# A second copy of K's high rows: by DMA, or by GpSimd from the first

## The reference

```
query = x @ Wq;  keyt = enc @ Wk;  valt = enc @ Wv          # 8 heads of 80
hs    = softmax(query keyt^T / sqrt(80)) valt               # per head, 100 x 718 scores
ca_q1 = (ca^T Wq_ca) at 100 picked rows
ca_hs1 = mha(ca_q1, x, x);  ca_q2 = ca_hs1 @ Wq
ca_hs2 = mha(ca_q2, ca @ Wk_ca, ca @ Wv_ca)                 # only 4 keys
out   = (hs + ca_hs2) @ Wout + b_out + x
```

## Time and profile before

| | |
|---|---|
| median of 3 runs | 1101.1 us (1098.77 to 1110.14) |
| span of the profiled execution, first to last instruction | 1101.6 us |
| time of the profiled execution as the profile has it | 1101.6 us (one core) |
| TensorE busy | 1036.2 us, 94% |
| VectorE, ScalarE busy | 668.4 us (61%), 490.6 us (45%) |
| GpSimd busy | 280.9 us (26%), 208 instructions |
| DMA by SyncE's queue | 181.63 MB, 72.3% of 16 engines' span |
| mean granted TensorE clock | 0.963 of full |

### The profile page before, as it was taken

How to read it: one execution, slowest core, us unless ns; L and a number is a source line. 1 busy time by engine, 2 the same in 40 slices (tenths; PEclk the granted TensorE clock), 3 DMA queues, 4 the chain that set the end, 5 groups by cost and what they waited for, 6 DMA issues and landing times.

```text
span 1101.6 us, 21261 instructions
## 1 busy us (share of the span) xinstructions
PE 1036.2 (94%) x7192; PEld 1011.9 (92%) x7192; DVE 668.4 (61%) x1138; ACT 490.6 (45%) x889; POOL 280.9 (26%) x208
## 2 busy tenths in 40 slices
PE   6998759999989899999999998999999999998998
PEld 5997749999989899999999998999999999898997
DVE  4444356676756656576656674667675676666344
ACT  4443243635454535354545453455544454445110
POOL 0000132323231322323233323142433151415000
PEclk9899779999999999899999998999998999999999
DMA  8676786767887969596969694869695969697255
GB/s 303 219 204 154 166 173 153 182 163 187 170 171 148 196 133 202 119 211 139 193 142 212 138 196 112 207 148 208 145 198 112 206 152 195 142 200 184 66 172 160
DMA packets 155050, 189.51 MB, mean 172 GB/s; under 512 B 78416, under 2 KB 108112, under 8 KB 155024
## 3 DMA queue, kind: packets, MB, share of 16 engines
q1 hardware_dynamic: 151696, 181.63, 72.3%
q10 hardware_dynamic: 3328, 7.54, 2.1%
HBM read 81.15 MB, written 19.74 MB: 92 GB/s over the span
## 4 chain that ended last, share of the span: by engine, by line
PE 70%; DMA 11%; SPq 4%; DVE 2%; ACT 1%; issue 1%; POOL 0%; DVEq 0%; ACTq 0%; POOLq 0%
PE psB L918 23%; PE psS L887 20%; DMA kstack<-kT_l 10%; PE psS L864 6%; PE psT L901 5%; PE psS L1022 4%; PE psT L941 4%; PE psT L947 2%; SPq L677 2%; PE psB L984 2%; SPq L674 1%; PE psB L1002 1%; DVE kT_l L1346 1%; PE psB L996 1%; PE psT L948 1%
## 5 line engine op out<-in xcount | busy, mean ns | idle before, releaser
L887 PE MATMUL psS<-encT_keep,Wk_keep 128*128 128x360 f32 x1440 | 264.1, 338 | 5.9 <-PEq L173 5.3
L887 PEld LDWEIGHTS psS<-encT_keep,Wk_keep 128*128 128x128 f32 x1440 | 247.4, 196 | 6.7 <-issue 5.3
L918 PE MATMUL psB<-PT_h,encN_h 120*128 120x400 f32 x576 | 203.7, 354 | 0.2 <-POOL encN_l L812 0.2
L918 PE MATMUL psB<-PT_l,encN_h 120*128 120x400 f32 x576 | 199.4, 346 | 0.0
L918 PE MATMUL psB<-PT_h,encN_l 120*128 120x400 f32 x576 | 198.5, 345 | 0.0
L1114 ACT ACTIVATE probs<-psS,negmax 100x718 f32<-100x718 f32 x128 | 110.4, 863 | 169.9 <-DVE negmax L1322 146.6
L1346 DVE TENSOR_TENSOR kT_l<-psS,kT_h 128x718 fp32r<-128x718 f32 x80 | 72.4, 905 | 112.0 <-ACT kT_h L1131 111.9
L1131 ACT ACTIVATE kT_h<-psS 128x718 fp32r<-128x718 f32 x80 | 61.7, 771 | 146.9 <-PE psS L887 137.0
L804 POOL TENSOR_TENSOR encT_keep<-encT_raw,encT_keep 128x718 fp32r<-128x718 f32 x45 | 79.4, 1763 | 181.5 <-ACT encT_keep L1137 179.1
L864 PE MATMUL psS<-kstack,qstack_h 120*100 120x360 f32 x256 | 90.7, 354 | 32.8 <-DMA kstack<-kT_l 27.0
L812 POOL TENSOR_TENSOR encN_l<-enc_raw,encN_h 120x768 fp32r<-120x768 f32 x48 | 90.7, 1889 | 116.3 <-ACT encN_h L1143 115.0
(11 more groups left out here) (143 smaller groups left out, 1868.4 us busy)
## 6 DMA issues: line engine op xcount, KB each, us to landing
kstack<-kT_h SPq DMA_DIRECT2D x64, 448.8 KB
kstack<-kT_l SPq DMA_DIRECT2D x192, 112.2 KB
enc_raw<-in_encN_dram SPq DMA_DIRECT2D x16, 1080.0 KB, 10.9
encT_raw<-in_encT_dram SPq DMA_DIRECT2D x15, 1077.0 KB, 8.5
kstack<-kT_h SPq DMA_DIRECT2D x32, 359.0 KB
kstack<-kT_h SPq DMA_DIRECT2D x32, 269.2 KB
kstack<-kT_h SPq DMA_DIRECT2D x32, 179.5 KB, 4.1
xT_raw<-in_xT_dram SPq DMA_DIRECT2D x4, 1000.0 KB, 7.8
```

The costliest lines, as they stand in the source:

```text
L887: mm = pe.matmul(keys_in(f, first)[:, half, 0:HALF], w[:, c, f * 128:(f + 1) * 128], e[:, c, k0:k0 + HALF], start=(j == 0), stop=(j == 3 * ...
L918: mm = pe.matmul(psB[:, 1, 0:RH], e[:, k, c * 128:(c + 1) * 128], a[:, k, half * RH:(half + 1) * RH], start=(j == 0), stop=(j == 3 * KT - 1))
```

## The change

One DMA per piece brings the high rows to plane 0 alone. GpSimd then copies the head's 80 high rows from plane 0 to plane 1, in the same partitions (`twice`), and TensorE waits for that copy instead of for the DMAs. The copies get places in GpSimd's written order; `encT_low` and `enc_low` are cut into their three parts so that copies can stand between them.

```diff
@@ lift (SyncE's queue)
-   high = kT[f % 2][0][a0:a0 + n, :].rearrange("p (o k) -> p o k", o=1)
-   sp.dma_start(raw(kst[r0:r0 + n, :, j, :]), raw(high.to_broadcast([n, 2, KEYS])))
+   sp.dma_start(raw(kst[r0:r0 + n, 0, j, :]), raw(kT[f % 2][0][a0:a0 + n, :]))
      .then_inc(s_lift[f, h], 16)
@@ GpSimd
+   def twice(b, h):
+       wait_lifted(pool, b + 1, h=h)
+       pool.sem_inc(s["passed_pool"], 1)
+       nc.gpsimd.tensor_copy(kst[0:D, 1, h % SLOTS, :], kst[0:D, 0, h % SLOTS, :]).then_inc(s["twice"], 1)
+       pool.wait_ge(s["twice"], HEADS * b + h + 1)
    spread_g(0, first=True)
+   twice(0, 0)
    split_x(0, first=True)
+   for h in (1, 2, 3):
+       twice(0, h)
    with pool.Fori(0, B - 1) as i:
-       encT_low(i + 1)
-       enc_low(i)
+       encT_low(i + 1, 0)
+       twice(i, 4)
+       encT_low(i + 1, 1)
+       twice(i, 5)
+       encT_low(i + 1, 2)
+       twice(i, 6)
+       enc_low(i, 0)
+       twice(i, 7)
+       enc_low(i, 1)
+       enc_low(i, 2)
        spread_v2(i)
+       twice(i + 1, 0)
        spread_g(i + 1)
+       twice(i + 1, 1)
        split_x(i + 1)
+       twice(i + 1, 2)
+       twice(i + 1, 3)
...
-   for c in range(3):
-       wo_low(c)
-   enc_low(B - 1)
+   twice(B - 1, 4)
+   wo_low(0)
+   twice(B - 1, 5)
+   wo_low(1)
+   wo_low(2)
+   twice(B - 1, 6)
+   enc_low(B - 1, 0)
+   twice(B - 1, 7)
+   enc_low(B - 1, 1)
+   enc_low(B - 1, 2)
@@ scores (TensorE)
-   wait_lifted(pe, i + 1, h=h)
+   pe.wait_ge(s["twice"], HEADS * i + h + 1)
```

More of the change, by code:

```diff
@@ L558, in attend @@
             c2copy c2add c2max c2sub c2sum c2inv c2norm p2lo clo csum cres ready"""
-        splits = "encT encN gbd ahi a xhi xlo v2bd wolo passed_sp passed_pool"
+        splits = "twice encT encN gbd ahi a xhi xlo v2bd wolo passed_sp passed_pool"
         names = " ".join((loads, products_done, exps_and_highs, steps_and_lows, splits)).split()
@@ L672, in lift @@
                         j = h % SLOTS
-                        high = kT[f % 2][0][a0:a0 + n, :].rearrange("p (o k) -> p o k", o=1)
-                        sp.dma_start(raw(kst[r0:r0 + n, :, j, :]), raw(high.to_broadcast([n, 2, KEYS])))\
+                        sp.dma_start(raw(kst[r0:r0 + n, 0, j, :]), raw(kT[f % 2][0][a0:a0 + n, :]))\
                           .then_inc(s_lift[f, h], 16)
@@ L798, in split_x, with encT_low, enc_low @@
                     pool.wait_ge(s["xlo"], b + 1)
[L801 to L814, removed]
+                def encT_low(b, c):
+                    pool.wait_ge(s["encThi"], PARTS * (b - 1) + c + 1)
+                    nc.gpsimd.tensor_tensor(eT[1][:, c, :], rawT[:, c, :], eT[0][:, c, :],
+                                            ALU.subtract).then_inc(s["encT"], 1)
+                    pool.wait_ge(s["encT"], PARTS * (b - 1) + c + 1)
+                def enc_low(b, c):
+                    ks = slice(c * KQ, (c + 1) * KQ)
+                    pool.wait_ge(s["encNhi"], PARTS * b + c + 1)
+                    nc.gpsimd.tensor_tensor(eN[1][:, ks, :], rawN[:, ks, :], eN[0][:, ks, :],
+                                            ALU.subtract).then_inc(s["encN"], 1)
+                    pool.wait_ge(s["encN"], PARTS * b + c + 1)
+                def twice(b, h):
[3 more added lines that the diff above has]
+                    pool.wait_ge(s["twice"], HEADS * b + h + 1)
                 def spread_v2(b):
```

## The result

The changed kernel takes 1120.3 us (median of 4, 1116.11 to 1122.88) against 1099.93 us (median of 4) for the kernel before: a ratio of 1.015, 95% interval 1.009 to 1.021. It is slower, as forecast, and inside the forecast range of 1100 to 1158, but by some 20 us and not by 36 to 38. The profiled execution has a span of 1121.1 us, 19.5 more than before.

The account below looks back on a forecast made before the run. TensorE, 94% busy, was taken as the bound at 53.35 us per middle batch; plus 2.8 delay and 2.4 clock, 14 batches gain 34.4 us. 1101.6 + 34.4 - 1 (first batch) + 3 (last) = 1138 us, range 1100 to 1158.

Parts of the forecast that it names:

- the wait at scores 5: In each middle batch TensorE waits for copy 5, queued on GpSimd behind two encT_low parts: 2.8 us late.
- the wait at head 6: TensorE's scores waiting for head 6's K DMAs; these waits all but vanish, at most 38.4 us won in the middle batches.
- The price of the clock behind the wait: Slower TensorE clock after the idle piece at scores 5: 2.4 us (0 to 4.6) added to each middle batch.
- The copy: One GpSimd copy of a head's high rows: 0.79 us, with 0.25 ahead and 0.1 to TensorE, 1.15 us.
- the low bound of the delay: Smallest lateness at scores 5 per batch, with copies of 0.72 us and no meeting with a normalization: 2.4 us.
- copy 6: GpSimd's copy for head 6, behind the third encT_low: done by 775.5, before its scores can start, costing nothing.
- VectorE's longer normalizations: Normalizations on VectorE lengthened by meeting copies: they have room before their turn, 0 us.
- The ends: Outside the middle batches: first batch -1 us, last batch +3, lead-in and projection 0.
- Heads 1, 2, 6 and 7: Copies for these heads in the middle batches: 0 us, with up to 0.8, 0.6 and 0.4 for heads 1, 2 and 7.
- Rival C: TensorE doesn't wait for copies 4 and 5 and all DMA waits go: 1063 us, chance 0.08.

Follow-up runs that it names:

- the run with late `x`: Changed kernel with its own order of copies 4 and 5, but copy 2 ahead of x's split and the split behind VectorE's low part of UT: 1108.14 us, ratio 1.007.

## Why the prediction was half right

**The mechanism** of the delay was right: the wait at scores 5, its place, its cause, its size for each batch, and that it takes the place of the wait at head 6. This is shown by the order of copies alone (1120 to 1066 us, and 1166 the other way). The price of the clock behind the wait was not right, and a second wait was missing.

**The copy**: 0.78 us beside 0.79 forecast; 0.19 and 0.34 us ahead of it (0.25); the delay is 2.45 us in a batch, 2.8 forecast, from several small terms: a low part of 1.73 instead of 1.82 us, 0.19 instead of 0.25 us ahead of copy 5, 0.05 instead of 0.1 us to TensorE. 14 x 0.35 = 4.9 us too much. Three slips in the working changed nothing: by its own terms the low bound of the delay is 2.5, not 2.4; copy 6 was timed without copy 5 ahead of it (measured, it ends at 729.70, and scores 6 start at 732.63); and the long casts of `x` in the kernel before, 1.44 us at 806.64, met VectorE's product of P and st (806.51 to 807.50, shown above) and not a normalization.

**The clock was the step that failed.** I took 2.4 us per wait, the mean over seven waits of 1.85 to 3.5 us, for a wait of about 2 us, and put it into every batch. Measured in the changed kernel: 811.1 - 14 x 53.35 - 14 x 2.45 - 9.7 = 20.2 us, 1.4 a batch; the clock fell behind 10 of 14 waits. 1.0 us a batch too much, 13.4 with the fractions. The kernel before had one wait at the same place, 1.85 us at 547.16, in this batch:

```profile
531.70:589.10 57.40, 54.93 (x388) 54.06 (x387) 36.51 (x64) 27.31 (x50) 17.87 (x12) 0.97 0.81 175
```

With 0.62 us of idle at scores 6 it leaves 57.40 - 53.35 - 1.85 - 0.62 = 1.6 us for the clock, which is what most falls cost in the changed kernel too; the mean of all seven hid it. With delays at scores 5 of about 0.6 us, and idle pieces of 1.95 and 3.8 us, the mean price was 0, 1.1 to 1.4 and 2.4 us. But length alone does not give the price: in the kernel before, waits of 2.22 and 2.35 us cost 3.1 and 4.6 us, two of 3.4 us cost 1.5 each, and one of 2.61 us nothing. What decides it for a single wait stays open.

**Values' wait for UT** was missed: +9.7 us. I had priced the earlier `x` only as a help for head 2 and VectorE's longer normalizations at nothing, because I looked only at who uses the normalized tile and not at what else is behind that instruction on VectorE.

**The ends**: +2 forecast, -6.3 measured. The first scores 2 come at 132.1 instead of 136.1 us, the first batch takes 2.9 us less, the last and the projection 0.6 more (3 forecast). TensorE's first K matmul in this stage starts at 106.6 instead of 109.7, so 3 of the 4 us at the start come from the stage ahead, which is the same code. It starts at 109.7 in the kernel before and in the one without copies, and at 105.4 to 107.0 in all ten profiled kernels with copies, whichever way the DMA writes; so chance between executions is not a likely cause. The cause stays open.

Together: 36.4 forecast on the span - 4.9 - 13.4 + 9.7 - 8.3 = 19.5, the measured difference.

Heads 1, 2, 6 and 7 cost nothing in the middle batches, as forecast. Rival C's time, 1063, is nearly what the same edit gives with copies 4 and 5 moved (1066).

## What to carry to other kernels

Work that is added to an idle engine is paid for by what stands ahead of it in that engine's order, not by the engine's busy share: put it ahead of anything that hangs on the consumer's own recent work. When a queue gets shorter, list what lands earlier and which engine it sets going then; a meeting of two engines at SBUF can move rather than vanish when a wait is added. Price a clock loss from a wait at the same place of the loop, where the trace has one, and not from the mean of all; and keep its range wide, since waits of 2.2 to 2.6 us cost 0 to 4.6 us in one trace here.

## What the runs showed of the hardware that was not expected

GpSimd's subtraction of `x` and VectorE's normalization or product followed each other rather than shared, and the one that started second paid: 0.60 us became 1.62 and 0.99 became 2.41, the excess 0.15 to 0.2 us less than what was left of GpSimd's 1.57; the other way round GpSimd's 1.57 became up to 2.42. VectorE's reduction of P took 0.97 us during a copy (646.49, copy from 646.37 to 647.21) and 0.98 in the kernel before, so this does not hold for every instruction of VectorE. That one split of `x`, off every critical path by itself, can cost TensorE up to 1.4 us a batch in this way was not expected.

Waits of 1.95 to 1.97 us at the same place of the same loop left the clock up in 4 of 14 batches and down in 10, in the run with late `x`, where only one batch held another wait (0.45 us).
